# Graph kernel on one core: the left sums as a column of H's products and a broadcast through DRAM, in place of their own products

## What is computed

```python
h = relu(layernorm(x))                       # input of block one, called hn here
type_sum = adj @ hn
attn_a = sigmoid(concat([type_sum, hn]) @ Wa.T + ba)      # attn_b alike
H = hn @ W_sa
s_left = H @ a_sa[:256]
s_right = H @ a_sa[256:]
e = where(adj != 0, exp(-leaky_relu(s_left[:, None] + s_right[None, :], 0.01)), 0)
x_a = (e / (e.sum(1) + 1e-5)) @ H
x_b = adj @ (hn @ W_gcnb) + b_gcnb
x = x + sigmoid(attn_a * x_a + attn_b * x_b)
```

## Time and profile before

| | us |
|---|---|
| median of 3 runs | 1598.15 |
| lowest, highest | 1597.79, 1599.51 |
| the profiled execution, its own time | 1598.0 |
| its span in the profile | 1596.2 |
| TensorE busy | 1552.2 (97%) |
| VectorE busy | 1140.6 (71%) |
| ScalarE busy | 1075.4 (67%) |
| GpSimd busy | 968.3 (61%) |
| TensorE's granted clock | 0.998 of 2.4 GHz |

### The profile page before, as it was taken

How to read it: one execution, slowest core, us unless ns; L and a number is a source line. 1 busy time by engine, 2 the same in 40 slices (tenths; PEclk the granted TensorE clock), 3 DMA queues, 4 the chain that set the end, 5 groups by cost and what they waited for, 6 DMA issues and landing times.

```text
span 1596.2 us, 34864 instructions
## 1 busy us (share of the span) xinstructions
PE 1552.2 (97%) x12946; PEld 1538.8 (96%) x12946; DVE 1140.6 (71%) x2145; ACT 1075.4 (67%) x2127; POOL 968.3 (61%) x864
## 2 busy tenths in 40 slices
PE   6999999999999999999999999999999999999996
PEld 5999999999999999999999999999999999999996
DVE  7766666766675677777777777756777777777773
ACT  4679989898985566666666666646666666666665
POOL 2112222222220488888888888847888888888884
PEclk9999999999999999999999999999999999999999
DMA  4124444544430133333333334522333333333333
GB/s 149 48 67 120 120 117 116 142 124 119 116 103 27 44 97 100 100 100 100 100 99 98 99 99 151 191 67 76 104 101 100 100 100 100 101 101 104 101 100 93
DMA packets 88666, 163.36 MB, mean 102 GB/s; under 512 B 9265, under 2 KB 19376, under 8 KB 88240
## 3 DMA queue, kind: packets, MB, share of 16 engines
q1 hardware_dynamic: 60624, 113.41, 24.2%
q0 software_dynamic: 24336, 44.31, 11.3%
q10 hardware_dynamic: 3536, 3.41, 0.7%
HBM read 147.99 MB, written 13.11 MB: 101 GB/s over the span
## 4 chain that ended last, share of the span: by engine, by line
PE 83%; issue 6%; DVE 5%; POOL 3%; ACT 2%; DMA 0%; SPq 0%; POOLq 0%; DVEq 0%; ACTq 0%
PE PS L1236 29%; PE PS L1448 8%; PE PS L1451 8%; PE PS L1450 8%; PE PS L1311 5%; PE PS L1308 5%; PE PS L1310 5%; PE PS L1309 5%; PE PS L1307 5%; POOL FR L467 2%; POOL X L460 1%; DVE AF L1052 1%; DVE AF L982 1%; ACT FR L650 1%; DVE PS L1092 1%
## 5 line engine op out<-in xcount | busy, mean ns | idle before, releaser
L467 POOL TENSOR_TENSOR FR<-AF,FR 128x512 fp32r<-128x512 f32 x338 | 451.7, 1336 | 139.0 <-ACT FR L650 134.1
L1236 PE MATMUL PS<-FR,RB 128*128 128x256 f32 x3900 | 515.9, 281 | 1.8 <-ACT X L616 1.8
L1236 PEld LDWEIGHTS PS<-FR,RB 128*128 128x128 f32 x3900 | 481.6, 188 | 3.1 <-ACT X L616 3.0
L460 POOL TENSOR_TENSOR X<-X,ROW 128x512 f32<-128x512 f32 x283 | 369.7, 1307 | 81.9 <-ACT ROW L660 81.9
L1448 PE MATMUL PS<-FR,RA 128*128 128x256 f32 x1300 | 372.7, 287 | 7.3 <-POOL FR L467 5.9
L1451 PE MATMUL PS<-FR,RA 128*128 128x256 f32 x1300 | 365.0, 281 | 0.0
L1450 PE MATMUL PS<-FR,RA 128*128 128x256 f32 x1300 | 364.3, 280 | 0.0
L1052 DVE TENSOR_TENSOR AF<-PS,AJ 128x512 f32<-128x512 f32 x338 | 231.4, 685 | 80.3 <-ACT PS L628 69.6
L425 POOL DMA_DIRECT2D STGT<-adjt x169 | 90.2, 534 | 292.9 <-PE PS L1311 292.9
L616 ACT ACTIVATE X<-PS 128x512 f32<-128x512 f32 x272 | 161.9, 595 | 142.2 <-DVE AF L982 136.8
L1448 PEld LDWEIGHTS PS<-FR,RA 128*128 128x128 f32 x1300 | 244.6, 188 | 13.3 <-POOL FR L467 11.7
(11 more groups left out here) (174 smaller groups left out, 2455.2 us busy)
## 6 DMA issues: line engine op xcount, KB each, us to landing
AJ<-adjt SPq DMA_DIRECT2D x338, 256.0 KB, 2.7
STGT<-adjt POOLq DMA_DIRECT2D x169, 256.0 KB, 3.0
xt_scratch<-ROW SPq DMA_DIRECT2D x12, 512.0 KB, 2.7
RB<-xt_scratch SPq DMA_DIRECT2D x12, 512.0 KB, 4.7
x_scratch<-X ACTq DMA_DIRECT2D x13, 256.0 KB, 2.1
ROW<-x_scratch SPq DMA_DIRECT2D x13, 256.0 KB, 3.1
out<-ROW SPq DMA_DIRECT2D x12, 256.0 KB, 3.3
X<-xt SPq DMA_DIRECT2D x1, 1536.0 KB, 11.5
```

The source lines that it names most:

```text
L460: nc.gpsimd.tensor_tensor(slot, slot, MB.unsqueeze(1).broadcast_to([P, 2, 256]), ALU.subtract)\
L467: nc.gpsimd.tensor_tensor(LO[g % 2], WA[g % 2], HI[g % 3].bitcast(F32), ALU.subtract)\
L1236: last = nc.tensor.matmul(out, stationary(a, k), moving(b, k), start=(k == 0 and i == 0), stop=(k == K - 1 and i == 2))
```

## The change

s_left of a node becomes one more column of H's products: the right sum W_sa a_right stays in column 258, W_sa a_left goes into column 259, which was a column of zeros. So `products_l`, `left_sums`, WSL and what builds it go away. VectorE's copy of the narrow columns (`h2_low`) takes four columns in place of three, and the fourth is SL, node by node on the partitions. To lie along the free dimension in every partition, SL makes a way through DRAM: SyncE waits until the tiles of a part are there (`sr_done`), stores them as one run of 256 or 1536 values (an element of 4 bytes for each descriptor on the SBUF side), waits for the store, and loads the run into all 128 partitions of SLB. There are three parts: pair 0, pairs 1 to 6, pairs 7 to 12. `leaky0` waits for the part of its pair (`sl_in`).

The sums W_sa a are taken by ScalarE's accumulator: four copies of 128x256 in place, with `accum_out` in the columns 258 and 259.

The turns in PSUM are five a pair; the transposes of pair 1 take bank 0. Unit 0 is moved: its leaky and exp come at the end of ScalarE's iteration 1, its high part, mask and low part in the iteration 2, ahead of those of unit 1. TensorE does it at the end of iteration 2, as before.

```diff
+SL_PARTS = [(0, 1), (1, 7), (7, PAIRS)]
...
+        sl_dram = nc.dram_tensor("sl_scratch", [T * P], F32).ap()
...
         def turn(pr, i):
-            return 6 * pr + i + 1 if i else max(6 * pr - 5, 0)
+            return 5 * pr + i + 1 if i else max(5 * pr - 4, 0)
 
         def bank_of(pr, i):
-            return 4 + turn(pr, i) % 4
+            return 0 if turn(pr, i) == 1 else 4 + turn(pr, i) % 4
...
             sp.dma_start(BIAS[:, :], rows[:, 2 * D:2 * D + GX]).then_inc(const_in, 16)
+            for i, (p0, p1) in enumerate(SL_PARTS):
+                sp.wait_ge(sr_done, 2 * p1)
+                sp.dma_start(sl_dram[2 * P * p0:2 * P * p1].rearrange("(t p o) -> p t o", p=P, o=1),
+                             SL[:, 2 * p0:2 * p1, :], allow_slow_non_contiguous=True).then_inc(sl_st, 16)
+                sp.wait_ge(sl_st, 16 * (i + 1))
+                sp.dma_start(SLB[:, 2 * P * p0:2 * P * p1],
+                             sl_dram[2 * P * p0:2 * P * p1].partition_broadcast(P)).then_inc(sl_in[i], 16)
...
-            def left_sums(pr):
-                act.wait_ge(sl_mm, pr + 1)
-                nc.scalar.activation(SLB[:, pr * 256:(pr + 1) * 256], PS[:, bank_of(pr, 1), 0:256], ACT.Copy)\
-                  .then_inc(slb_done, 1)
...
             def leaky0(n):
                 pr, u = n // UNITS, n % UNITS
-                act.wait_ge(slb_done, pr + 1)
+                act.wait_ge(sl_in[next(i for i, (p0, p1) in enumerate(SL_PARTS) if pr < p1)], 16)
...
-            act.wait_ge(wv_step, 1)
-            nc.scalar.activation(WSL[:, 0, :, :], WV[:, 0, :].unsqueeze(2).broadcast_to([P, K, P]), ACT.Copy)\
-              .then_inc(wsl_hi, 1)
-            act.wait_ge(wv_step, 3)
+            for side in range(2):
+
+                act.wait_ge(wv_pool, side + 1)
+                c = GX + D + 3 - side
+                for k in range(K):
+                    wa = (PEB, PAB)[side][:, k, 0:D]
+                    last = nc.scalar.activation(wa, wa, ACT.Copy, accum_out=WRAW0[:, k, c:c + 1])
+            last.then_inc(wv_done, 1)
+            act.wait_ge(wv_done, 1)
             act.wait_ge(wv_zero, 1)
             nc.scalar.activation(WX[:, 0, :, GX:WC], WRAW0[:, :, GX:WC], ACT.Copy).then_inc(wh_cast, 1)
             for p in range(PAIRS):
                 if 1 <= p < PAIRS - 1:
                     transposed_high(p + 1)
-                if p >= 1:
+                if p == 2:
+                    high0(0)
+                if p >= 2:
                     leaky0(p - 1)
-                    left_sums(p)
                     exp0(p - 1)
                 g_high(p, 0)
                 g_high(p, 1)
                 if p == 0:
                     transposed_high(1)
-                    left_sums(0)
-                if p >= 1:
+                if p >= 2:
                     high0(p - 1)
                 h2_high(p, 0)
                 h2_high(p, 1)
+                if p == 1:
+                    leaky0(0)
+                    exp0(0)
...
-                nc.vector.tensor_copy(XS[:, t, 0:3], PS[:, bank_of(pr, 4 + h), D:D + 3]).then_inc(sr_done, 1)
+                nc.vector.tensor_copy(XS[:, t, :], PS[:, bank_of(pr, 3 + h), D:D + 4]).then_inc(sr_done, 1)
...
             transposed_low(0)
-            dve.wait_ge(wv_pool, 1)
-            nc.vector.reduce_sum(WV[:, 0, :], PEB[:, :, 0:D], AX).then_inc(wv_step, 1)
             scales(1, 2, 6)
             normalise(1)
-            dve.wait_ge(wv_pool, 2)
-            nc.vector.reduce_sum(WV[:, 1, :], PAB[:, :, 0:D], AX).then_inc(wv_step, 1)
-            dve.wait_ge(wv_step, 2)
-            nc.vector.tensor_copy(WRAW0[:, :, GX + D + 2:GX + D + 3], WV[:, 1, :].unsqueeze(2)).then_inc(wv_step, 1)
-            dve.wait_ge(wsl_hi, 1)
-            nc.vector.tensor_tensor(WSL[:, 1, :, :], WV[:, 0, :].unsqueeze(2).broadcast_to([P, K, P]),
-                                    WSL[:, 0, :, :].bitcast(F32), ALU.subtract).then_inc(w_ready, 1)
             dve.wait_ge(wh_cast, 1)
...
             for p in range(PAIRS):
                 if 1 <= p < PAIRS - 1:
                     transposed_low(p + 1)
+                if p == 2:
+                    mask0(0)
...
                 g_low(p, 0)
-                if p >= 1:
+                if p == 2:
+                    low0(0)
+                if p >= 2:
                     mask0(p - 1)
                 g_low(p, 1)
...
                 h2_low(p, 0)
-                if p >= 1:
+                if p >= 2:
                     low0(p - 1)
...
                 pe.wait_ge(htlo_done, p + 1)
-                if p >= 1:
-                    products_l(p)
                 products_g(p)
                 if p == 0:
                     transpose0(1)
-                    pe.wait_ge(w_ready, 2)
-                    products_l(0)
+                    pe.wait_ge(w_ready, 1)
                 products_h(p)
```

More of the change, by code:

```diff
@@ L140, in two_graph_blocks @@
         HT = [FR[:, i:i + 2, :].rearrange("p s (k n) -> p s k n", k=K) for i in (4, 6)]
-        WSL = FR[:, 8, :].rearrange("p (s k c) -> p s k c", s=2, k=K)
         AJ = sb("AJ", [P, 2 * WC + 2 * D], F32)
@@ L193, in two_graph_blocks @@
         wv_zero = sem("wv_zero")
-        wv_step = sem("wv_step")
-        wsl_hi = sem("wsl_hi")
+        wv_done = sem("wv_done")
+        sl_st = sem("sl_st")
+        sl_in = [sem(f"sl_in{i}") for i in range(len(SL_PARTS))]
         wh_cast = sem("wh_cast")
@@ L434, in _ @@
             pool.wait_ge(w_in, 16)
-            nc.gpsimd.memset(WRAW0[:, :, GX + D + 3:WC], 0.0).then_inc(wv_zero, 1)
+            nc.gpsimd.memset(WRAW0[:, :, GX + D + 4:WC], 0.0).then_inc(wv_zero, 1)
             pool.wait_ge(row_in, 16)
@@ L498, in h2_high @@
                 act.wait_ge(h2_mm, 2 * pr + h + 1)
-                nc.scalar.activation(RA[:, 2 * pr + h, 0:D], PS[:, bank_of(pr, 4 + h), 0:D], ACT.Copy)\
+                nc.scalar.activation(RA[:, 2 * pr + h, 0:D], PS[:, bank_of(pr, 3 + h), 0:D], ACT.Copy)\
                   .then_inc(h2hi_done, 1)
@@ L1247, in projected @@
                 else:
-                    q, j = (i - 1) // 6, (i - 1) % 6
+                    q, j = (i - 1) // 5, (i - 1) % 5
+                    if j == 0 and q == 0:
+                        return
                     if j == 0:
                         pe.wait_ge(htlo_done, q + 2)
-                    elif j == 1:
-                        pe.wait_ge(slb_done, q + 1)
-                    elif j < 4:
-                        pe.wait_ge(glo_done, 2 * q + j - 1)
+                    elif j < 3:
+                        pe.wait_ge(glo_done, 2 * q + j)
                     else:
-                        pe.wait_ge(h2lo_done, 2 * q + j - 3)
+                        pe.wait_ge(h2lo_done, 2 * q + j - 2)
             def transpose0(pr):
@@ L1265, in transpose0 @@
                 last.then_inc(tp_done, 1)
-            def products_l(pr):
-                ht = HT[pr % 2]
-                projected(turn(pr, 1))
-                product3(PS[:, bank_of(pr, 1), 0:256], lambda a, k: WSL[:, a, k, :], lambda c, k: ht[:, c, k, :])\
-                    .then_inc(sl_mm, 1)
             def products_g(pr):
@@ L1275, in products_g @@
                 for h in range(2):
-                    projected(turn(pr, 2 + h))
-                    product3(PS[:, bank_of(pr, 2 + h), 0:GX], lambda a, k: ht[:, a, k, h * P:(h + 1) * P],
+                    projected(turn(pr, 1 + h))
+                    product3(PS[:, bank_of(pr, 1 + h), 0:GX], lambda a, k: ht[:, a, k, h * P:(h + 1) * P],
                              lambda c, k: WX[:, c, k, 0:GX]).then_inc(g_mm, 1)
@@ L1282, in products_h @@
                 for h in range(2):
-                    projected(turn(pr, 4 + h))
-                    product3(PS[:, bank_of(pr, 4 + h), 0:HX], lambda a, k: ht[:, a, k, h * P:(h + 1) * P],
+                    projected(turn(pr, 3 + h))
+                    product3(PS[:, bank_of(pr, 3 + h), 0:HX], lambda a, k: ht[:, a, k, h * P:(h + 1) * P],
                              lambda c, k: WX[:, c, k, GX:GX + HX]).then_inc(h2_mm, 1)
```

11 lines of the change are left out of this document (4 added, 7 removed).

## The result

| | before | after |
|---|---|---|
| median of 20 runs, us | 1598.48 | 1600.61 |
| lowest, highest | 1597.5, 1599.87 | 1599.67, 1602.95 |
| the profiled execution, its own time | 1598.0 | 1599.91 |
| its span | 1596.2 | 1598.1 |

The ratio of the times is 1.0014, with a 95% interval of 1.0008 to 1.0021: 0.14% slower, within the 0.2% that counts as no change here. The forecast was 1593.1 us, in a range up to 1596.6; all 20 runs lie above it.

The account below looks back on a forecast made before the run. The kernel was taken as TensorE-bound, its front first paced by VectorE, with gains counted at unit 12's start: 0.4 + 1.9 + 2.1 + 0.6 = 5.0 us, giving 1593.1 us, range 1590.0 to 1596.6.

Parts of the forecast that it names:

- The way through DRAM, first part: Pair 0's store and load at the start: taken as 6.5 us, arriving at 24.2 us, 0.55 us lost.
- A first leaky behind 25 us: Listed sign of a wrong forecast: ScalarE's first leaky, expected near 24.2 us behind the load, starting after 25 us.
- its point of 23.65 us: Arrival of the first load early enough for pair 3's low part, which VectorE wants at 25.6 us.
- my rival at 0.14: First way through DRAM takes 10.9 us, 4.85 us lost in place of 0.55: 1597.4 us, chance 0.14.
- The third part: Last store and load, asked for by unit 13 near 95 us: 18 us with the load, hidden under 35 us.
- The slower case: Store of 1536 single values decides from about 0.3 us a packet; at 0.5 us, 1612 us; chance 0.05.
- The end of iteration 2: In the front, VectorE was to be 0.95 us ahead there, before the loss to the way through DRAM.
- The head: VectorE's start: 1.21 us of work goes, next statistics start at 17.9 us instead of 19.76, 1.9 us gained.
- The wait for G's copy in iteration 2: VectorE waits 1.6 us for ScalarE's copy of G; over iterations 1 and 2, 0.95 us given back.
- Iterations 4 to 7: H's second product of iteration 7 starts at 63.3 us, not 65.2: 1.9 us gained, 0.8 from H's order.
- TensorE's 0.71 us an iteration: L's six matmuls go from TensorE, 0.71 us an iteration; iterations 8 to 10 counted for 2.1 us.
- The end of the front: From the transposes to unit 12, `left_sums` leaves the chain twice: 0.6 us gained; wait grows to about 2.8 us.

Follow-up runs that it names:

- e2: The changed kernel with all three parts of the left sums loaded from input x and no stores (so other scores): 1594.69 us, ratio 0.9972 to its own before.
- e10: The changed kernel with the first part stored and loaded as rows of 8 bytes, leaky taking every second value: 1596.33 us, ratio 0.9983 to its own before.
- e1: The changed kernel with only pair 0's left sums loaded early from input x, without their store (other scores): 1594.94 us, ratio 0.9974 to its own before.
- e3: The changed kernel with the third part's store and load delayed until unit 51's leaky, near 200 us: 1604.4 us, ratio 1.0037 to its own before.
- e4: The changed kernel with ScalarE's and VectorE's work for units 0 and 1 moved to the end of iteration 2: 1597.2 us, ratio 0.9988 to its own before.
- e4b: The edits of e4 and e3 together on the changed kernel: 1601.6 us, ratio 1.0016 to its own before.
- e5: The changed kernel plus six scratch stores, one after another: 256, 128, 512 single values; 128 rows of 32, 128, 8 bytes. Single run 1601.4 us.
- e7: The changed kernel plus four scratch stores: 128 side-by-side single values, 256 and 1536 rows of 8 bytes, 256 single values issued by GpSimd. Single run 1601.32 us.

## Why the prediction was wrong, step by step

- **The way through DRAM, first part: the step that failed.** Taken 6.5 us, measured 7.4 + 3.8 = 11.2 us. I priced the store by its packets, at 0.10 us each, and took the queue's start from a store of 256 KB. The probes show a fixed piece of some 4 us for rows of one value that no row of before has. The first leaky came at 29.11 us, not at 24.2; in place of 0.55 us, 4.39 + 1.03 = 5.4 us were lost against e2. A first leaky behind 25 us was my sign of being wrong. The mechanism itself was right, with its point of 23.65 us (23.75 by the prediction's own terms, 25.6 - 1.3 - 0.55): 29.11 - 23.65 = 5.46 us against the 5.42 lost, and in e10 25.66 - 23.65 = 2.01 us against 1.03 + 1.03 = 2.06. Only the size of the way was off. The upper bound, 10.9 us, was my rival at 0.14; it priced the loss at 4.85 us.
- **The third part: put at nothing, and the reason was wrong.** I asked only whether its values come in time (they do: ScalarE never waits for the loads of the parts 2 and 3). Of the adjacency I wrote that GpSimd's queue isn't touched and has six units, 14 us, of lead. In the trace of before VectorE wants a tile 7.6 us after its load is issued at 100.5 us, and 4.3 us after it at 189.3 us, and beside the store such a load takes up to 12.4 us. The store costs 1.2 us after and 1.3 in e1, nothing in e2, where it isn't made, and 6.3 us where it stands behind the front. The slower case needed 0.3 us a packet; the longest of these stores, 12.8 us, is 0.13 us for each of its 96 an engine.
- **The rest of the sum: three terms held, one was too high.** With the way for nothing the sum is 0.95 + 1.9 + 2.1 + 0.6 = 5.55 us, and e2 has 4.98 at unit 12. The terms can be read one by one. The end of iteration 2 was to be 0.95 us ahead: unit 0 is at -1.03. The head: statistics at 18.10 us, 17.9 forecast. The wait for G's copy in iteration 2: 1.78 us, 1.6 forecast. Iterations 4 to 7: 1.2 us (units 1 to 5 in e2, from -1.28 to -2.44), 1.9 forecast; this term was 0.7 us too high. TensorE's 0.71 us an iteration: 3.5 us over five (units 5 to 10), 3.55 forecast. The end of the front: from the transposes to unit 12 it is 105.02 - 88.49 = 16.53 us, before 16.96, so 0.43 us for 0.6; the wait there is 2.53 us for 2.8. Unit 12 starts at 99.61 us in e2, 99.6 forecast, which is luck: the forecast has 0.55 us of loss in it that e2 hasn't, and the term that was too high makes up for it.
- **The account.** 5.0 us of gain (e2), less 5.4 for the first part and 1.2 for the third, is 1.6 us lost at unit 16; the profiled executions differ by 1.9 us, the medians by 2.1.
- **A page's rule.** The Trainium skill (DMA: Bandwidth & Descriptors, Rules for kernel authors) speaks against a non-contiguous last dimension, and in direction the trace agrees (7.4 us for 1 KB). Its fit, made for transfers that GpSimd issues, gave 4.3 us for both ways as an estimate; measured 11.2. The line that the same page's Specifications draw at 512 bytes doesn't show here as a longer time to landing: rows of 8, 32 and 128 bytes took 2.8, 1.5 and 2.9 us.

Still open: what happens in the fixed piece. In the window from 20 to 23 us the DMA engines are idle (share 0.00) while the first store is under way; its packets are seen only from 23 to 24 us. How the store holds up the loads of another queue is open too: only its place in time was tried, not the third part in rows of 8 bytes. And the way through DRAM isn't equally long in every execution: 11.1 to 12.5 us from the store's issue to the first leaky in the traces of after, e3, e4, e4b, e5 and e7.

## What to carry to other kernels

Price a DMA by the shape of its rows, and measure that shape alone before a chain is hung on it: here one neighbour more in the row (8 bytes for 4) made the store 4.4 us faster. Count a load's lead from its issue to the first engine that reads the tile, not in buffers. Ask of every transfer what it does to the queues beside it, even if nobody waits for it. A column of per-partition values is laid over all partitions more cheaply by one transpose of its broadcast view than by a way through DRAM, where TensorE has that time.
